# Top-k attention: result copy moved behind the next exponent, and row maximum and steep threshold ahead of the flag's load

## What is computed

```python
scores = einsum('bhnd,bhmd->bhnm', q, k) * 32 ** -0.5
kth = top_k(scores, 64)[0][..., -1:]
masked = where(scores >= kth, scores, finfo.min)
attn = softmax(masked, axis=-1)
o = einsum('bhnm,bhmd->bhnd', attn, v)
```

## Time and profile before

| what | value |
|---|---|
| median of 3 runs | 5078.21 us (5076.14 to 5078.52) |
| the profiled execution | 5075.16 us, span 5073.4 us |
| granted TensorE clock, whole span | 0.837 |
| VectorE busy, whole span | 4332.4 us, 85% |
| ScalarE busy, whole span | 4161.6 us, 82% |
| TensorE matmul busy, whole span | 4120.5 us, 81% |
| GpSimd busy, whole span | 1502.7 us, 30% |
| VectorE busy, 500 to 2900 us | 2295.89 of 2400 us |
| ScalarE busy, 500 to 2900 us | 2215.34 of 2400 us |
| TensorE matmul busy, 500 to 2900 us | 1746.26 of 2400 us |
| GpSimd busy, 500 to 2900 us | 1144.59 of 2400 us |

### The profile page before, as it was taken

The page is one execution under the profiler, slowest core; times in us unless marked ns, Lnnn a source line. Parts: engine busy times, 40 slices in busy tenths (PEclk is TensorE's granted clock), DMA queues, the critical chain, the costliest instruction groups (busy, mean ns, idle before and its releaser), DMA issues. The chain is left out here.

```text
span 5073.4 us, 107203 instructions
## 1 busy us (share of the span) xinstructions
PE 4120.5 (81%) x32161; PEld 2777.1 (55%) x32161; DVE 4332.4 (85%) x25624; ACT 4161.6 (82%) x6082; POOL 1502.7 (30%) x362
## 2 busy tenths in 40 slices
PE   8576677777777676777777777898999999999999
PEld 4344445544555444454554445444567777777776
DVE  3999999999999999999999999431378888888886
ACT  2799799999999799999999899544268888888885
POOL 0344445444455444444444444100100000000000
PEclk9777777777777777777777777899899999999999
DMA  6000000000000000000000000200420101111112
GB/s 217 7 18 17 7 17 17 9 17 16 9 18 17 7 17 8 18 18 8 18 18 17 9 17 11 64 6 0 157 73 25 34 25 34 27 32 34 25 34 95
DMA packets 79598, 154.63 MB, mean 30 GB/s; under 512 B 8120, under 2 KB 49464, under 8 KB 73528
## 3 DMA queue, kind: packets, MB, share of 16 engines
q1 hardware_dynamic: 78904, 146.72, 10.1%
HBM read 99.50 MB, written 47.19 MB: 29 GB/s over the span
## 5 line engine op out<-in xcount | busy, mean ns | idle before, releaser
L542 POOL TENSOR_TENSOR a_probs<-a_scores,a_probs 128x2304 f32<-128x2304 f32 x288 | 1460.6, 5092 | 1623.8 <-ACT a_probs L465 1623.8
L560 DVE MAX8 a_top<-a_scores 128x8 f32<-128x36 f32 x18432 | 1832.5, 182 | 31.9 <-ACT a_scores L449 23.4
L376 PE MATMUL a_ps_t<-ident,a_probs 128*128 128x128 f32 x5184 | 964.0, 322 | 521.1 <-ACT a_probs_t L460 378.5
L376 PEld LDWEIGHTS a_ps_t<-ident,a_probs 128*128 128x128 f32 x5184 | 666.7, 163 | 815.0 <-ACT a_probs_t L460 519.6
L1300 DVE TENSOR_SCALAR_CACHE_REDUCE b_soft<-b_ps_s 128x2304 f32<-128x2304 f32 x288 | 735.2, 2553 | 26.2 <-PE b_ps_s L1159 8.5
L465 ACT ACTIVATE a_probs<-a_scores,a_steep_kth 128x2304 f32<-128x2304 f32 x290 | 641.3, 2212 | 136.2 <-DVE a_minus_max L700 136.1
L460 ACT ACTIVATE a_probs_t<-a_ps_t 128x512 f32<-128x512 f32 (+1 forms) x1440 | 728.9, 548 | 14.8 <-PE a_ps_t L376 3.2
L1175 PE MATMUL b_ps_t<-ident,b_soft 128*128 128x128 f32 x5184 | 727.0, 276 | 1.6 <-DVE b_soft_t L1306 0.6
L1175 PEld LDWEIGHTS b_ps_t<-ident,b_soft 128*128 128x128 f32 x5184 | 577.2, 140 | 170.1 <-ACT b_soft_t L1264 60.1
L453 ACT ACTIVATE a_probs<-a_probs,a_minus_max 128x2304 f32<-128x2304 f32 x288 | 638.1, 2216 | 31.8 <-issue 18.1
L366 PE MATMUL a_ps_s<-a_k_stack,a_q_ring 128*128 128x512 f32 (+1 forms) x1465 | 650.8, 604 | 16.1 <-ACT a_scores L449 10.7
(11 more groups left out here) (133 smaller groups left out, 4135.9 us busy)
## 6 DMA issues: line engine op xcount, KB each, us to landing
a_k_stack<-k_parts SPq DMA_DIRECT2D x72, 288.0 KB, 6.0
b_k_stack<-k_parts SPq DMA_DIRECT2D x72, 288.0 KB, 6.0
a_q_ring<-q_parts SPq DMA_DIRECT2D x294, 64.0 KB
b_q_ring<-q_parts SPq DMA_DIRECT2D x294, 64.0 KB
k_parts<-p_high SPq DMA_DIRECT2D x36, 256.0 KB, 2.0
...
```

The lines of the kernel that those rows point to most:

```text
L376: last = pe.transpose(ps_t[(NTG * s + g) % 2][:, P * m:P * m + P], probs[s % 2][:, P * (m0 + m):P * (m0 + m) + P], cst["ident"][:, :])
L542: pool.tensor_tensor(probs[u][:, :], scores_all[:, 2 * (p % 2) + u, :], probs[u][:, :], ALU.subtract).then_inc(masked_ready, 1)
L560: last = dve.max(top8[s // 2 % 2][:, s % 2, c, :], scores_all[:, s % 4, CHUNK * c:CHUNK * c + CHUNK])
```

## The change

Three edits, in `attention_top` alone.

1. On ScalarE, the exponent of the next pair's first tile is written ahead of `finish`, not behind it. The first exponent of all stands ahead of the loop, and the loop runs over seven heads, with the eighth written out behind it, since its last pair has no next exponent.
2. On VectorE, the largest eighth value of a row is taken with a MAX8 for each tile in `prepare`, in place of one reduction that gave both row maximum and largest eighth value.
3. Also on VectorE, the steep threshold and a reduction for the row maximum are issued behind the wait for the flag and ahead of its load. Minus the maximum follows the branch, with a wait of its own (`first_ready`). A search is preceded by a drain and followed by a second computation of the steep threshold.

```diff
--- before.py
+++ after.py
@@ -295,7 +295,8 @@
         factor, guess = sb("factor", [P, 2]), sb("guess", [P, 2])
         above_guess, place = sb("above_guess", [P, 2]), sb("place", [P, 2])
         places, picked = sb("places", [P, WINDOW]), sb("picked", [P, 2, WINDOW])
-        extremes, eighths, beyond = sb("extremes", [P, 2, 2]), sb("eighths", [P, 2]), sb("beyond", [P, 2])
+        first_of_row, beyond = sb("first_of_row", [P, 2]), sb("beyond", [P, 2])
+        eighths, rest_eighths = sb("eighths", [P, 2, 8]), sb("rest_eighths", [P, 2])
         doubt = sb("doubt", [P, 2])
         flag, flag_t, flags = sb("flag", [P, D]), sb("flag_t", [P, D]), sb("flags", [1, P])
         any_doubt, any_above = sb("any_doubt", [1, 3], I32), sb("any_above", [1, 1], I32)
@@ -315,7 +316,7 @@
         tops_taken, dve_order = sem("tops_taken"), sem("dve_order")
         first_guessed, balance_ready = sem("first_guessed"), sem("balance_ready")
         doubt_ready, doubt_counted, any_ready = sem("doubt_ready"), sem("doubt_counted"), sem("any_ready")
-        kth_ready = sem("kth_ready")
+        first_ready, kth_ready = sem("first_ready"), sem("kth_ready")
         penalty_ready, masked_ready, probs_ready = sem("penalty_ready"), sem("masked_ready"), sem("probs_ready")
         turned, turned_kept = sem("turned"), sem("turned_kept")
         weighed, parts_ready, added, o_kept = sem("weighed"), sem("parts_ready"), sem("added"), sem("o_kept")
@@ -449,9 +450,10 @@
                 act.activation(scores_all[:, s % 4, :], ps_s[:, 0:N], ACT.Copy).then_inc(scores_kept, 1)
 
             def exponentials(s, h, tile, parity):
+                ahead, s = divmod(s, HEAD_TILES)
                 act.wait_ge(masked_ready, tile + 1)
                 act.activation(probs[s % 2][:, :], probs[s % 2][:, :], ACT.Exp, scale=SCALE,
-                               bias=minus_max[parity][:, s % 2:s % 2 + 1], accum_out=sums[:, s, cols(h, 1)]
+                               bias=minus_max[parity][:, s % 2:s % 2 + 1], accum_out=sums[:, s, cols(h + ahead, 1)]
                                ).then_inc(probs_ready, 1)
 
             def keep_turned(s, g, tile):
@@ -499,32 +501,40 @@
             for u in range(2):
                 penalty(u, 0)
             guess_place(0, 1, 1)
-            with act.Fori(0, HEADS) as h:
+            exponentials(0, 0, 0, 0)
+
+            def pair_step(p, h, last=False):
+                pair, tile, s, parity = h * HEAD_PAIRS + p, h * HEAD_TILES + 2 * p, 2 * p, p % 2
+                keep_scores(s + 4, tile + 4)
+                guess_place(1, pair + 1, 1 - parity)
+                keep_turned(s, 0, tile)
+                keep_turned(s, 1, tile)
+                exponentials(s + 1, h, tile + 1, parity)
+                keep_turned(s, 2, tile)
+                keep_turned(s, 3, tile)
+                keep_turned(s, 4, tile)
+                keep_scores(s + 5, tile + 5)
+                keep_any(pair + 1)
+                keep_turned(s + 1, 0, tile + 1)
+                keep_turned(s + 1, 1, tile + 1)
+                act.wait_ge(kth_ready, pair + 2)
+                penalty(0, 1 - parity)
+                keep_turned(s + 1, 2, tile + 1)
+                keep_turned(s + 1, 3, tile + 1)
+                keep_turned(s + 1, 4, tile + 1)
+                penalty(1, 1 - parity)
+                act.wait_ge(weighed, tile + MCH + 3)
+                act.activation(parts[:, :], ps_o[:, 0:PAIR], ACT.Copy).then_inc(parts_ready, 1)
+                guess_place(0, pair + 2, parity)
+                if not last:
+                    exponentials(s + 2, h, tile + 2, 1 - parity)
+                finish(s, h, pair)
+
+            with act.Fori(0, HEADS - 1) as h:
                 for p in range(HEAD_PAIRS):
-                    pair, tile, s, parity = h * HEAD_PAIRS + p, h * HEAD_TILES + 2 * p, 2 * p, p % 2
-                    exponentials(s, h, tile, parity)
-                    keep_scores(s + 4, tile + 4)
-                    guess_place(1, pair + 1, 1 - parity)
-                    keep_turned(s, 0, tile)
-                    keep_turned(s, 1, tile)
-                    exponentials(s + 1, h, tile + 1, parity)
-                    keep_turned(s, 2, tile)
-                    keep_turned(s, 3, tile)
-                    keep_turned(s, 4, tile)
-                    keep_scores(s + 5, tile + 5)
-                    keep_any(pair + 1)
-                    keep_turned(s + 1, 0, tile + 1)
-                    keep_turned(s + 1, 1, tile + 1)
-                    act.wait_ge(kth_ready, pair + 2)
-                    penalty(0, 1 - parity)
-                    keep_turned(s + 1, 2, tile + 1)
-                    keep_turned(s + 1, 3, tile + 1)
-                    keep_turned(s + 1, 4, tile + 1)
-                    penalty(1, 1 - parity)
-                    act.wait_ge(weighed, tile + MCH + 3)
-                    act.activation(parts[:, :], ps_o[:, 0:PAIR], ACT.Copy).then_inc(parts_ready, 1)
-                    guess_place(0, pair + 2, parity)
-                    finish(s, h, pair)
+                    pair_step(p, h)
+            for p in range(HEAD_PAIRS):
+                pair_step(p, HEADS - 1, last=p == HEAD_PAIRS - 1)
 
         @block.gpsimd
         def _(pool):
@@ -568,14 +578,11 @@
 
             def prepare(pair, tops):
 
-                wait_alone(dve, tops_taken, 2 * pair + 1)
-                counted(rest_of_half(tops, 0, 0))
-                counted(rest_of_half(tops, 0, 1))
-                wait_alone(dve, tops_taken, 2 * pair + 2)
-                counted(rest_of_half(tops, 1, 0))
-                counted(rest_of_half(tops, 1, 1))
-                counted(dve.tensor_reduce(extremes[:, :, :], tops[:, :, 0:CHUNKS, 0:8:7].rearrange("p u c k -> p u k c"),
-                                          AX.X, ALU.max))
+                for u in range(2):
+                    wait_alone(dve, tops_taken, 2 * pair + u + 1)
+                    counted(rest_of_half(tops, u, 0))
+                    counted(rest_of_half(tops, u, 1))
+                    counted(dve.max(eighths[:, u, :], tops[:, u, 0:CHUNKS, 7]))
 
             def select(pair, tops):
 
@@ -594,7 +601,7 @@
                 guesses = counted(dve.tensor_tensor(guess[:, :], factor[:, :], minus_first[:, :], ALU.mult))
                 after(guesses)
                 written = [0, 0]
-                counted(dve.tensor_tensor(eighths[:, :], tops[:, :, CHUNKS + REST - 1, 0],
+                counted(dve.tensor_tensor(rest_eighths[:, :], tops[:, :, CHUNKS + REST - 1, 0],
                                           tops[:, :, CHUNKS + REST - 1, 1], ALU.max))
                 for u in range(2):
                     rows = counted(dve.tensor_scalar(below_of(u), candidates(u), guess[:, u:u + 1], None, ALU.is_ge,
@@ -604,7 +611,7 @@
                     written[u] = counted(dve.scalar_tensor_tensor(below_of(u), candidates(u), guess[:, u:u + 1],
                                                                   candidates(u), ALU.is_lt, ALU.mult))
                 counted(dve.tensor_scalar(place[:, :], above_guess[:, :], -1.0, TOPK - 1.0, ALU.mult, ALU.add))
-                counted(dve.tensor_tensor(beyond[:, :], extremes[:, :, 1], eighths[:, :], ALU.max))
+                counted(dve.tensor_tensor(beyond[:, :], eighths[:, :, 0], rest_eighths[:, :], ALU.max))
                 for r in range(WINDOW // 8):
                     found = [0, 0]
                     for u in range(2):
@@ -695,22 +702,28 @@
                             rounds_again(parity, u)
                 dve.drain()
 
-            def give_kth(parity):
-                dve.tensor_scalar(steep_kth[parity][:, :], kth[:, :], STEEP, None, ALU.mult)
-                dve.tensor_scalar(minus_max[parity][:, :], extremes[:, :, 0], -SCALE, None,
-                                  ALU.mult).then_inc(kth_ready, 1)
-
-            def load_doubt(pair):
+            def steepen(parity):
+                return dve.tensor_scalar(steep_kth[parity][:, :], kth[:, :], STEEP, None, ALU.mult)
+
+            def hand_on(pair, parity):
+
+
+
+
                 after(at["n"])
                 dve.sem_clear(dve_order)
                 at["n"] = 0
                 wait_alone(dve, any_ready, pair + 1)
-                return dve.value_load(any_doubt[0:1, 2:3])
-
-            def hand_on(pair, parity):
-                with dve.If(load_doubt(pair) > 0):
+                steepen(parity)
+                dve.tensor_reduce(first_of_row[:, :], top8[parity][:, :, 0:CHUNKS, 0], AX.X,
+                                  ALU.max).then_inc(first_ready, 1)
+                with dve.If(dve.value_load(any_doubt[0:1, 2:3]) > 0):
+                    dve.drain()
                     search_again(parity)
-                give_kth(parity)
+                    steepen(parity)
+                dve.wait_ge(first_ready, pair + 1)
+                dve.tensor_scalar(minus_max[parity][:, :], first_of_row[:, :], -SCALE, None,
```

(1 more changed line is left out.)

## The result

| | before | after |
|---|---|---|
| median of the runs compared (7 each) | 5078.21 us | **5095.53 us** (5094.18 to 5097.26) |
| ratio, with its 95% interval | | **1.0036** [1.0027, 1.0045] |
| the profiled execution | 5075.16 us, span 5073.4 | 5096.6 us, span 5094.8 |
| granted TensorE clock, whole span | 0.837 | 0.841 |
| first to last `minus_max` start | 139.8 to 3194.1 us | 140.0 to 3212.9 us |

The change makes the kernel slower by 17.3 us, and all of it lies in the top-k stage: 144 `minus_max` now span 3072.9 us, not 3054.3, which is 18.6 more.

The account below looks back on a forecast made before the run. The prediction took a ring through four engines (kth ready, penalty, GpSimd, exponent, score copy, guess, selection, flag) as the bound. Its terms, 15.0 - 7.3 + 0 + 2 + 4.4 = +14.1, gave 5092 us, range 5066 to 5115.

Parts of the forecast that it names:

- the likeliest case: Whole kernel: slower, at 5092 us, given 5080 to 5106; chance 0.52.
- `finish` behind the exponent: ScalarE, between exponent and score copy: the results' copy adds 0.12 in each of 125 pairs, +15.0 us.
- The signs given: Trace: exponent 0.13 behind GpSimd, idle there about 0.5 a pair, `finish` without a wait, plain pair about 20.64 us.
- The path from exponent to flag: Top-k pair: exponent, score copy, guess, VectorE's selection, doubt, TensorE's count, its copy and flag follow without slack.
- Head ends: ScalarE's loop turn: earlier exponent saves 0.8 at six ends, -4.8, and 2.5 at the eighth head's start; together -7.3 us.
- VectorE ahead of selection: VectorE's `prepare`: MAX8s replacing the reduction free 0 to 0.3 us a pair, but that shortens nothing: 0.
- "faster" rival: VectorE's work ahead of selection sets the pace, so 0.3 less counts in each pair: 5035 us; chance 0.13.
- VectorE at the flag: Flag to `minus_max`: plain pairs gain 0.03, some 20 quick-jump pairs lose about 0.25; together +2 us.
- Searches: VectorE's search start: a drain waiting for the reduction costs 0.4 in each of 11 searches, +4.4 us.
- Same: Rival: head ends give their full 2.0 each and `finish` costs 0.10, 5081 us; chance 0.24.
- No overlap on VectorE: Rival at the flag: steep value and reduction don't overlap, `minus_max` 0.17 late in 125 pairs, 5113 us; chance 0.06.
- The load waits for the reduction: Rival at the flag: its load starts only after the reduction, 0.8 in each of 125 pairs, 5190 us; chance 0.05.

Follow-up runs that it names:

- number 1: Kernel before with only ScalarE's program from the change (exponent ahead of `finish`, seven heads looped, one written out); 5084.97 us, ratio 1.0016.
- number 6: Changed kernel with the copy of the results done twice, behind the exponent; 5122.53 us, ratio 1.0081.
- number 7: Kernel before with the copy of the results done twice, ahead of the exponent; 5079.34 us, ratio 0.9999.
- number 8: Kernel before, order unchanged, with ScalarE's loop over seven heads and the eighth written out; 5074.19 us, ratio 0.9994.
- number 9: Kernel before, order unchanged, with all eight heads of ScalarE's program written out; 5062.27 us, ratio 0.9970.
- number 3: Kernel before with only the new `prepare` (largest eighth values by MAX8, row maximum reduced there), flag step as before; 5078.57 us, ratio 0.9998.
- number 4: Kernel before with only the new flag step, `prepare` as before; 5085.89 us, ratio 1.001.
- number 5: Kernel before with VectorE's part of the change, but its row-maximum reduction right behind the doubt and the flag step four MAX8s earlier; 5077.1 us, ratio 1.0.

## Why the prediction was right, step by step

The forecast was 5092 with a range of 5066 to 5115; it was 5095.5, and slower, as the likeliest case said. Terms against the stage times, the sum being +14.1 against +18.6. It came as near as that partly because the misses have both signs: head ends gave less, searches and quick jumps cost more, and late selections and the last head gave what nobody had counted.

- **`finish` behind the exponent, +15.0.** Right in mechanism, place and size: 0.10 to 0.12 in each pair (numbers 1 and 6, and nothing in number 7), the exponent still 0.13 behind GpSimd. The signs given all came: no wait at `finish`, idle time put down to GpSimd (70.7 over 113 pairs, 0.63 each, where I said 0.5), plain pair 20.66 where I said 20.64. Over the whole stage the distance from exponent to score copy grows by 14. Unforeseen is position 10, where the exponent comes 0.41 behind GpSimd (the wait of 0.9 in the list above) and costs 0.28 more, in each of the seven looped heads, with the copy alone as well. Its register instruction ran on time and the exponent itself came late. I take that for instructions not there yet, by where the code lies. No run was made for it, but number 6 moves all later code of ScalarE by having the copy twice in each pair, and there all seven exponents of position 10 are back at 0.13. What the delay costs, 1.9, the last head nearly gives back with its 0.10 a pair (number 8).
- **The path from exponent to flag.** The prediction led it over guess, VectorE's selection and TensorE's count "without slack". That step was off by 0.05. ScalarE's second score copy and its copy of the count, in the plain pair before:

```profile
1531.72 2.09 ACT L449 ACTIVATE a_scores<-a_ps_s 128x2304 f32<-128x2304 f32 x1
1533.69 0.15 ACT L470 ACTIVATE a_any_doubt<-a_ps_o 1x3 f32<-1x3 f32 x1
```

The copy of the count follows the score copy in ScalarE's own queue after 1.97 (so in 84 of the 108 pairs of the second to seventh head), and between the exponent at 1522.09 and this copy ScalarE stands idle for 0.07 in all. Selection and count run beside it with 0.05 to spare: the copy of the count stands 0.43 behind the doubt, and where selection is late (positions 2 and 7) it stands 0.38 behind, and the pair loses 0.20 to 0.30 for a selection 0.25 to 0.35 late. For `finish` the price is the same, as it lies on both paths. But by these rows a faster selection alone would have given nothing, and whatever is put between exponent and count copy on ScalarE is paid as well; neither was run.
- **Head ends, -4.8 and -2.5.** The direction and the limit were right: VectorE's own loop decides. Mis-sized: -2.2, not -4.8, that is 0.37 and not 0.8 each. The timelines of ScalarE and VectorE at the head's end that the earlier trace rows show before:

```profile
937.67 2.09 ACT L450 ACTIVATE a_scores<-a_ps_s 128x2304 f32<-128x2304 f32 x1 [0.65 <-issue]
```

```profile
941.19 0.88 DVE L570 MAX8 a_top<-a_scores 128x8 f32<-128x36 f32 x8 [2.37 <-issue]
```

The scores are there at 939.8, but VectorE's loop (L750, before L737) starts its new turn only later:

```profile
L750 DVEq COMPARE_BRANCH  x1: 63/63/63, 937.9 to 937.9; - x1
L750 DVEq FUSED_REGOPS  x1: 63/63/63, 941.0 to 941.0; - x1
```

Before, the first instruction of the turn came at 934.1 and the wait ended at 935.02; I took all 0.9 of that for the gain, less 0.1. But the first MAX8 stands 0.2 behind the first instruction, so only 0.7 were there (0.59 in the mean of the six ends), and the way from VectorE's branch to that instruction was longer: 3.1 here, where it had been 2.7, and in the mean of the six ends 2.96 and not 2.81. Why it was longer stays open; with VectorE's program unchanged it was 2.82 in numbers 8 and 9 and 2.92 in numbers 1 and 7. The last 0.08 were lost from selection to `minus_max`, which takes 7.44 there where it took 7.36 (with the copy alone, so without VectorE's new flag step, 7.19). So 0.59 - 0.15 - 0.08 is the 0.37, but for rounding. With the copy alone the head ends gave -4.0. The last head's start was -3.0 where I said -2.5; leaving a loop into written-out code stalled nobody (20.55).
- **VectorE ahead of selection, 0.** Right: 36.8 us in 106 waits for the score copy where there had been 19.1 in 13; plain pair 20.54 with VectorE's part alone. The "faster" rival (VectorE sets the pace, 5035) is refuted by that.
- **VectorE at the flag, +2.** The reduction is 382 ns, as taken (0.38). A quick jump loses by it what was said: `minus_max` stands 0.04 behind the reduction's end, and the shortest pairs take 20.44 with VectorE's part alone and not 20.22, so 0.22 where I said 0.25. Mis-sized was the plain pair, whose gain of 0.03 isn't there: the flag's load comes 0.36 behind the copy of the count and not 0.28, which eats the 0.08 of the steep value. And quick jumps got fewer as they moved: 19 before, without the heads' starts, and 14 after. Together the way from the copy of the count to `minus_max` costs 4.1 in the pairs without a search, heads' starts left out. (The +5.3 to +5.7 in the experiments are those of the old positions, where the jump is no longer quick; positions 9 and 14 give a part of it back.) Against that stand -2.5 where selection had been late (positions 2 and 7). That gain comes with number 3 too (-2.2), whose flag step is as before, and with number 4 (-2.8), whose `prepare` is, and in number 5 the late selection stands at position 6 instead. So it goes with where the code lies, as far as these runs show.
- **Searches, +4.4.** The mechanism (a drain behind the reduction) was right; 0.59 each and not 0.40: 0.11 of `finish`, 0.08 of the later load and 0.4 of the drain (1.47 from the branch to the first work, before 1.08). I had counted only the last.
- **The rivals.** *Same* (5081) needed 2.0 at each head's end; it was 0.37. *No overlap on VectorE* (5113) didn't come: the reduction starts 0.06 behind the steep value of 0.15, so the rule that the prediction cites from the Trainium skill, "VectorE: DVE Perf Modes", section "The DRAIN you can't avoid", does not describe what two instructions in a row do here. The section itself adds what the prediction left out, that a next operation starts earlier where it isn't held, so made to wait for all earlier ones; the 0.06 agrees with that. *The load waits for the reduction* (5190) didn't come: the load of the search starts at 1183.6 and the reduction, by the drain, ends near 1184.4.
